# Attention over gathered edge rows: GpSimd's waits between groups of gathers count three of four landings, and one wait more stands between two batches

## The reference

```python
k_e = k[src]; q_e = q[dst]; v_e = v[src]
kw = _typed_rel(k_e, rel_att, etype)
a = (kw * q_e).sum(-1) * rel_pri.T[etype] / jnp.sqrt(jnp.float32(D))
m = _typed_rel(v_e, rel_msg, etype)
amax = jax.lax.stop_gradient(jax.ops.segment_max(a, dst, num_segments=N))
ex = jnp.exp(a - amax[dst])
den = jax.ops.segment_sum(ex, dst, num_segments=N)
attn = ex / jnp.maximum(den[dst], 1e-09)
h = jax.ops.segment_sum(m * attn[:, :, None], dst, num_segments=N).reshape(N, DIM)
```

## Time and profile before

| | us |
|---|---|
| median of three runs | 4584.94 |
| the runs | 4579.43 to 4593.61 |
| the profiled execution | 4592.19 |
| its span in the trace | 4590.3 |
| POOL busy in it | 2411.3 (53%) |
| PE busy in it | 2969.0 (65%) |
| DVE busy in it | 2312.5 (50%) |

### The profile page before, as it was taken

One profiled execution on the slowest core, in us unless ns is written; L12 is line 12 of the kernel. 1 busy time (PEld: TensorE's weight loads), 2 busy tenths in 40 slices (PEclk: granted clock), 3 DMA queues, 4 the chain that ended last, 5 costly groups with the idle time before them and its releaser, 6 DMA issues. The chain is left out here.

```text
span 4590.3 us, 52237 instructions
## 1 busy us (share of the span) xinstructions
PE 2969.0 (65%) x14449; PEld 2143.5 (47%) x14449; DVE 2312.5 (50%) x8186; ACT 1147.0 (25%) x2512; POOL 2411.3 (53%) x2514
## 2 busy tenths in 40 slices
PE   3895666666676666664420666777767776767774
PEld 3774656666666656663200433344433444433342
DVE  3774655655655555553522345533455534455435
ACT  1223556555655555552001200000000000000001
POOL 0002544444466666665577266665466664666662
PEclk9998778777787877776755889988899988999987
DMA  4896555565422322221000455555545545555552
GB/s 110 273 358 232 199 200 210 189 216 191 163 88 80 87 79 81 84 81 48 1 1 0 172 190 174 189 191 184 186 174 190 189 174 179 192 188 176 189 189 61
DMA packets 232026, 706.47 MB, mean 154 GB/s; under 512 B 62326, under 2 KB 111957, under 8 KB 212928
## 3 DMA queue, kind: packets, MB, share of 16 engines
q1 hardware_dynamic: 104252, 447.79, 26.7%
q0 software_dynamic: 93184, 191.21, 14.4%
q10 hardware_dynamic: 34308, 64.13, 4.3%
HBM read 559.66 MB, written 143.28 MB: 153 GB/s over the span
## 5 line engine op out<-in xcount | busy, mean ns | idle before, releaser
L552 POOL DMA_INDIRECT stage<-h_tab,earr x1248 | 1183.3, 948 | 810.8 <-issue 346.5
L527 POOL DMA_INDIRECT arena<-kv_tab,idxr x832 | 796.0, 957 | 970.3 <-ACT idxr L634 405.6
L1013 PE MATMUL bank<-arena,xr 128*128 128x512 f32 (+1 forms) x2058 | 1021.1, 638 | 5.6 <-issue 5.6
L992 PE MATMUL bank<-oh,stage 128*128 128x128 f32 x2496 | 394.3, 308 | 494.0 <-issue 487.8
L992 PEld LDWEIGHTS bank<-oh,stage 128*128 128x128 f32 x2496 | 354.1, 214 | 712.3 <-issue 701.1
L860 PE MATMUL bank<-xr,arena 128*128 x3328 | 494.0, 308 | 236.8 <-DVE arena L1254 146.9
L1572 DVE TENSOR_TENSOR sums<-sums,bank 128x128 f32 x1248 | 351.3, 282 | 568.3 <-remote 398.2
L1013 PEld LDWEIGHTS bank<-arena,xr 128*128 128x128 f32 x2058 | 407.6, 212 | 394.8 <-issue 394.8
L860 PEld LDWEIGHTS bank<-xr,arena 128*128 128x128 f32 x3328 | 456.0, 218 | 259.3 <-issue 258.2
L499 POOL DMA_INDIRECT a_tab<-tot,cell x416 | 416.0, 1000 | 261.2 <-DMA arena<-kv_tab,idxr 151.1
L709 ACT ACTIVATE rs<-mv,epsc 128x49 f32<-128x49 f32 (+1 forms) x6 | 1.9, 316 | 2003.3 <-DVE mv L1611 1692.6
(11 more groups left out here) (224 smaller groups left out, 2739.4 us busy)
## 6 DMA issues: line engine op xcount, KB each, us to landing
arena<-a_tab SPq DMA_DIRECT2D x147, 1792.0 KB
a_tab<-stage SPq DMA_DIRECT2D x49, 1792.0 KB
kv_tab<-stage SPq DMA_DIRECT2D x48, 768.0 KB, 8.5
arena<-key_d ACTq DMA_DIRECT2D x52, 512.0 KB, 7.1
arena<-ew_d ACTq DMA_DIRECT2D x52, 512.0 KB, 10.1
arena<-rel_d SPq DMA_DIRECT2D x52, 512.0 KB
stage<-h_tab,earr POOLq DMA_INDIRECT x1248
arena<-kv_tab,idxr POOLq DMA_INDIRECT x832
```

What stands on the lines that cost most here:

```text
L527: G.indirect_dma_start(kv[b % 3][:, t, :], None, kv_tab, bass.IndirectOffsetOnAxis(idxr[:, b % 3, t:t + 1], 0))\
L552: G.indirect_dma_start(gring[:, (q % NG) * GRP + s, :], None, h_tab[l], bass.IndirectOffsetOnAxis(src_i[:, t:t + 1], 0)).then_inc(row_land ...
L992: last = M.matmul(bank[q % NG][:, s * P:(s + 1) * P], gring[:, (q % NG) * GRP + s, :], oh[:, q % NG, s, :], start=True, stop=True)
L1013: mm = M.matmul(o_[:, 0:cw], xr[:, n, :], abuf[B % NBUF][:, n % KB, 0:cw], start=n == 0, stop=n == NT - 1)
```

## The change

A group's first three gathers still raise `kv_land`, which so reaches 48 a batch. The fourth raises a semaphore of its own, `kv_last[n % 2]`, where n = 4b + g counts the groups through all batches. POOL now waits before every group but the very first, so between two batches too, for the first three gathers of the group before; and from the third group on for the fourth gather of the group before last. DVE and ACT, which need all four, wait on both semaphores. No instruction changes its place on any engine, and the same gathers and scatters are issued.

```diff
--- before.py
+++ after.py
@@ -261,6 +261,7 @@
         idx_ready = sem("idx_ready")
         gathers_begun = sem("gathers_begun")
         kv_land = [[sem(f"kv_land{a}_{g}") for g in range(NG)] for a in range(3)]
+        kv_last = [sem(f"kv_last{a}") for a in range(2)]
         rel_in = [sem(f"rel_in{a}") for a in range(2)]
         neg_in = [sem(f"neg_in{a}") for a in range(2)]
         act_link = sem("act_link")
@@ -515,8 +516,12 @@
                     for j in range(ND):
                         pool.wait_ge(a_zeroed[j], 16 * BPC)
                 for g in range(NG):
-                    if g:
-                        pool.wait_ge(kv_land[b % 3][g - 1], 64 * (b // 3 + 1))
+                    n = NG * b + g
+                    if n:
+                        b_, g_ = (n - 1) // NG, (n - 1) % NG
+                        pool.wait_ge(kv_land[b_ % 3][g_], 48 * (b_ // 3 + 1))
+                    if n >= 2:
+                        pool.wait_ge(kv_last[n % 2], 16 * (n // 2))
                     for t in slots.get((b, g), ()):
                         scatter(t)
                     if b >= 3:
@@ -526,7 +531,7 @@
                         t = g * GRP + s
                         G.indirect_dma_start(kv[b % 3][:, t, :], None, kv_tab,
                                              bass.IndirectOffsetOnAxis(idxr[:, b % 3, t:t + 1], 0))\
-                         .then_inc(kv_land[b % 3][g], 16)
+                         .then_inc(kv_land[b % 3][g] if s < GRP - 1 else kv_last[n % 2], 16)
             for b in range(NB):
                 gather(b)
             for t in range(first_of, first_of + SY):
@@ -630,7 +635,9 @@
             def indices(b):
                 if b >= 3:
                     for g in range(NG):
-                        act.wait_ge(kv_land[b % 3][g], 64 * (b // 3))
+                        act.wait_ge(kv_land[b % 3][g], 48 * (b // 3))
+                    for a in range(2):
+                        act.wait_ge(kv_last[a], 16 * (NG // 2) * (b - 2))
                 S.activation(idxr[:, b % 3, :], idx_c[:, bass.ds(b * TPB, TPB)], ACT.Copy).then_inc(idx_ready, 1)
 
             def one_hot_T(b, i, par, g):
@@ -1241,7 +1248,8 @@
 
             def products(b, i, par, g):
 
-                dve.wait_ge(kv_land[b % 3][g], 64 * (b // 3 + 1))
+                dve.wait_ge(kv_land[b % 3][g], 48 * (b // 3 + 1))
+                dve.wait_ge(kv_last[g % 2], 16 * ((NG * b + g) // 2 + 1))
                 dve.wait_ge(q_done, NG * b + g + 1)
                 kg = kv[b % 3][:, g * GRP:(g + 1) * GRP, 0:D]
                 dl.inc(V.tensor_tensor(kg, kg, bank[g % 2][:, :].rearrange("p (s f) -> p s f", s=GRP), ALU.mult))
```

## The result

The changed kernel takes 4803.9 us (median of 4 runs, 4802.2 to 4810.5) where the kernel before takes 4586.8 (4579.4 to 4593.6): a ratio of 1.0475, 95% interval 1.0462 to 1.0488. It is **slower by 217 us**, where 130 less were forecast; 4803.9 lies above the whole range of 4390 to 4645. The span of the profiled execution grew from 4590.3 to 4802.6.

The account below looks back on a forecast made before the run. POOL's gathers and its waits for their landings were taken to set the pace, DVE following. Gains of 10 + 67 + 53 = 130 us from 4592.2 gave 4462, less 7.2 for the median: 4455 us, range 4390 to 4645.

Parts of the forecast that it names:

- Three landings in place of four: Before groups 1, 2 and 3, POOL's wait ends about 1.25 us earlier: 195 us gained.
- the price of the new wait: POOL's new wait before group 0 costs 0.5 or 1.05 us more per batch: 40 us.
- the collision: POOL's wait of about 7.0 us before group 2 in batches 3 to 25, where gathers meet SP's loads and zero fills.
- The first half, 67 + 10: Batches 3 to 27 gain 25 x 2.69 = 67 us, the first three batches 10 us.
- the collision wait falls by 2.5 in the loop: First half, from SP's feed to POOL's next group 2: 12.19 - 2.5 = 9.7 us, making a loop of 28.9.
- What is late next, the second half: From batch 28, DVE's path lies between 29.3 and 33.6 us; a period of 31.6 against 33.8 gains 53 us.
- late signals: PE's signals reach DVE late, in gaps of POOL's DMA stream; DVE waited 38.95 us at the end of attention.
- The tail: What follows attention starts from its last scatter and moves as a block, with no gain or loss of its own.
- Rival C: Gaps of 0.8 and 1.35 us are too short for PE's signals to DVE: +30 to +182 us, chance 0.22.
- waits for the next gap, a group later: A PE-to-DVE hand-off that misses its gap waits 6.05 us in the first half, 7.6 in the second.
- The rule of the Trainium skill: DMA queues alternate by packets, so gathers beside fills are slowed, not held: wait before group 2 near 2.6, change bringing 1.25.

Follow-up runs that it names:

- e2: The changed kernel without the wait for a landing between two batches, three of four inside a batch: 4722.0 us, 1.0327 of the kernel before.
- h2: The kernel before without POOL's waits for landings from batch 28 on, run on the fourth chip: 4170.3 us, 0.9596 of the kernel before.
- f3: The changed kernel with two increments of an unread semaphore behind the landing waits from batch 28 on: 4566.6 us, 0.9958 of the kernel before.
- f1: The kernel before without POOL's waits for landings from batch 28 on, run on the second chip: 4897.1 us, 1.0674 of the kernel before.
- e1: The changed kernel, but POOL waits before every group, between batches too, for all four gathers: 4767.6 us, 1.0433 of the kernel before.
- e3: The changed kernel in batches 0 to 27 only; from 28 on POOL waits as in the kernel before, with the new semaphores: 4569.0 us, 0.9994.
- g1: The kernel before, from batch 28 on without landing waits but with two unread increments before each group, third chip: 4161.2 us, 0.9588.
- g2: The kernel before, from batch 28 on without landing waits but with eight unread increments before each group, third chip: 4159.0 us, 0.9587.

## Why the prediction was wrong

By its steps:

- **Three landings in place of four, and the price of the new wait**: right. Gaps of 0.8 in the second half and 1.35 in the first, 5.8 at the collision, in both traces of the changed kernel; the wait before group 3 alone did not follow.
- **The first half, 67 + 10**: right in sign, too large. 30 came on the chip of the result and 39 on the other sort. Most of the missing part stands before group 3, where the median wait stayed at 2.5: 25 x 1.2 = 30 us; what holds the gathers of group 2 there was not tried. Another 10 is the stop of 11.75 before batch 3, for DVE; on the other sort of chip it was 1.4. e2 adds that without the wait between batches it would have been 60. The step that the collision wait falls by 2.5 in the loop is not borne out: it fell by 1.2.
- **What is late next, the second half**: this is the step that failed. I took DVE's path as 29.3 to 33.6, read off two pairs of rows of the old cadence, as if it were a fixed length into which the new gaps would fit. The late signals, which I had read correctly in the earlier trace rows, were not a length but a function of the very gaps that the change shortens: at 0.8 they hold DVE at the chain until POOL stops by itself. 44 a batch came (42.9 in the mean), against 31.6: a loss of 208 us where the term stood at a gain of 53.
- **The tail**, put at nothing ("What follows attention starts from its last scatter and moves as a block"), also failed. It starts from y_set, and y_set waits for DVE and its late signals: 39.9 us were lost there. A row of the prediction's own stands in that tail.
- **Rival C** had the mechanism and the point from which it decides ("more than 0.8 us of silence"), and a price of 36.9 a batch that was too small by 7 (44 measured in the steady state). The mis-sized term is "waits for the next gap, a group later": with all gaps too short there is no next one, only POOL's stop three batches on, once a batch. What I wrote against C, that POOL would stop and so make long gaps again, is true and is the state in which the kernel runs: 29.9 of POOL's run and 14.4 of stop. I gave it 0.22; with 38.95 us behind a stream without gaps in the earlier trace rows and no row of a signal within 0.8, I now think that it deserved more than the forecast. Its total of +30 to +182 is still short of the 217 measured, since neither the steady stop nor the tail is in it.
- **The rule of the Trainium skill** on the DMA queues ("DMA: Bandwidth & Descriptors", section "Queues, rings and completion order"): the wait at the collision was 7.0 and with the change 5.8, as the row would have it, on both sorts of chip, and in the two batches before the scatters that have no fills beside them it was 2.8 and 2.6. The rule as I read it, a delay by the gather's share alone, does not give that. The section speaks of turns by packets, and how long the fills' packets hold a turn was not looked at.
- **What I could not see**: the whole premise, late signals, belongs to the chip on which the trace was taken, or to its state. On the other sort the change brought 153 us where 130 were forecast, with a second half at 30.9, near POOL's own pace of 30.5. That the totals are so close is luck: the first half gave 39 in place of 77 and the second 106 in place of 53, from a start of 35.6 a batch and not of 33.8.

## What to carry to other kernels

When one engine's waits are shortened, ask what else uses these waits: here many of TensorE's late signals reached VectorE and ScalarE in the idle gaps of GpSimd's DMA stream, and a wait that is only bookkeeping for one engine was breathing space for three. A rival that ends on the other side should be priced at its steady state (who stops whom, and once per what), not as one more delay. And a result that hangs on how signals travel should be taken on more than one chip: this change is 4.75% slower on one and 3.6% faster on another.

## What the runs showed of the hardware

- On the chip of the first trace a semaphore that TensorE raised changed late while GpSimd issued indirect DMAs 0.30 us apart: in the tail of the kernel before VectorE stood 38.95 us and went on 39.5 after the matmul had ended. On the fourth chip it went on 0.03 us after the same matmul, and in h2, amid 22 such DMAs, 0.03 us too. The kernel before takes 4571 and 4588 on two chips with the delay (4587 in the first result) and 4338 and 4344 on two without.
- In the changed kernel, where the delay shows, TensorE started a matmul of 0.37 us only every 1.44 beside the DMAs, and nine of them took 2.08 us behind the last.
- On chips with the delay, gaps of 0.8, 1.46 and 1.77 us after every four to six DMAs gave 44, 33.4 and 34.9 us a batch, and no gap at all 46. Where between 0.8 and 1.46 it turns was not measured.
- Signals that were late and came in a gap came 1.6 us (median) after GpSimd's last DMA in the kernel before, 1.3 in f3, 1.9 in the changed kernel and 3.8 in f1, behind 22 DMAs without a gap.
- Where GpSimd waited for a third landing and then for the fourth, its next DMA came 2.6 us after the last one's issue had ended, against 2.07 with one wait (e1 and e3, second half). Two increments behind the waits lengthened a gap of 0.80 to 1.46, and four more to 1.77, 0.08 each. With no wait before them, two or eight increments left the pause at 0.30 (g1, g2).
